# A decoder's row norms: statistics of four token sets per row group instead of two

## What is computed

```python
def _layernorm(x, axis=-1, eps=1e-05):
    m = jnp.mean(x, axis=axis, keepdims=True)
    v = jnp.var(x, axis=axis, keepdims=True)
    return (x - m) / jnp.sqrt(v + eps)
...
    x = x + _L0_attn_ref(_layernorm(x, axis=-1), ...)
    x = x + _L0_xattn_ref(_layernorm(x, axis=-1), ctx_1024, ...)
    x = x + _L0_ffn_ref(_layernorm(x, axis=-1), ...)
...
    x = x + _L3_ffn_ref(_layernorm(x, axis=-1), ...)
```

## Time and profile before

| | us |
|---|---|
| median of 3 runs | 2486.11 (2483.11 to 2487.94) |
| the profiled execution | 2487.08 |
| its span in the trace | 2485.0 |
| PE busy | 1851.5 (75%) |
| DVE busy | 1760.5 (71%) |
| ACT busy | 1120.0 (45%) |
| POOL busy | 707.7 (28%) |

### The profile page before, as it was taken

How to read it: one execution, slowest core, us unless ns; L and a number is a source line. 1 busy time by engine, 2 the same in 40 slices (tenths; PEclk the granted TensorE clock), 3 DMA queues, 4 the chain that set the end, 5 groups by cost and what they waited for, 6 DMA issues and landing times. The chain is left out here.

```text
span 2485.0 us, 36889 instructions
## 1 busy us (share of the span) xinstructions
PE 1851.5 (75%) x11751; PEld 1096.4 (44%) x11763; DVE 1760.5 (71%) x5601; ACT 1120.0 (45%) x3109; POOL 707.7 (28%) x617
## 2 busy tenths in 40 slices
PE   6996889962887999979887875666555555556778
PEld 2654446441354766644454543333333333333343
DVE  4336352268775666657745778999999999997665
ACT  3653442251315777731232554555555555554411
POOL 1200044005433333310032421344333333331130
PEclk7998899976998999989997897666665665667979
DMA  5000000310000000000100000000000000000000
GB/s 214 2 1 1 29 26 27 104 65 1 2 2 1 2 2 1 0 1 0 72 24 1 1 1 1 1 1 1 1 1 1 1 1 1 1 1 1 1 0 18
DMA packets 10591, 37.76 MB, mean 15 GB/s; under 512 B 1344, under 2 KB 7488, under 8 KB 9136
## 3 DMA queue, kind: packets, MB, share of 16 engines
q1 hardware_dynamic: 8880, 33.04, 3.4%
q0 software_dynamic: 1536, 2.59, 0.4%
HBM read 30.15 MB, written 5.51 MB: 14 GB/s over the span
## 5 line engine op out<-in xcount | busy, mean ns | idle before, releaser
L3733 PE MATMUL psum<-work 32*128 32x256 f32 x512 | 130.3, 653 | 288.2 <-ACT work L3851 288.2
L3913 DVE MATCH_REPLACE8 work<-work 128x256 f32<-128x256 f32 x768 | 322.1, 497 | 0.0
L3976 POOL TENSOR_TENSOR work<-work 128x1024 f32<-128x1024 f32 x63 | 148.3, 2355 | 484.2 <-ACT work L3851 484.2
L3910 DVE MAX8 work<-work 128x8 f32<-128x256 f32 x768 | 283.0, 495 | 0.0
L3733 PEld LDWEIGHTS psum<-work 32*128 32x128 f32 x512 | 77.8, 310 | 314.4 <-ACT work L3851 159.1
L718 POOL TENSOR_TENSOR work<-work 128x256 f32<-128x256 f32 (+2 forms) x144 | 133.5, 946 | 226.2 <-DVE work L1006 226.2
L934 ACT ACTIVATE work<-work 128x128 f32<-128x128 f32 (+1 forms) x320 | 145.3, 457 | 19.9 <-DVE work L981 18.2
L3851 ACT ACTIVATE work<-work 128x256 f32<-128x256 f32 x256 | 129.0, 504 | 0.0
L3913 DVE MATCH_VALUE_LOAD work<-work 128x8 f32 x768 | 128.0, 167 | 0.0
L3758 PE MATMUL psum<-work,tiles 128*8 128x256 f32 x512 | 116.9, 609 | 8.2 <-ACT work L3861 7.4
L3978 POOL TENSOR_TENSOR work<-work 128x1024 f32<-128x1024 f32 x63 | 119.3, 1894 | 6.0 <-DVE work L3935 1.2
(11 more groups left out here) (621 smaller groups left out, 4647.3 us busy)
## 6 DMA issues: line engine op xcount, KB each, us to landing
big_weights<-L0f_dram SPq DMA_DIRECT2D x1, 6117.5 KB, 28.5
big_weights<-L_dram SPq DMA_DIRECT2D x1, 5772.0 KB, 17.1
big_weights<-L_dram SPq DMA_DIRECT2D x1, 4952.5 KB, 16.1
choice_rows<-tiles SPq DMA_DIRECT2D x2, 1024.0 KB, 10.2
tiles<-choice_rows SPq DMA_DIRECT2D x8, 256.0 KB, 4.9
big_weights<-L_dram SPq DMA_DIRECT2D x1, 2027.0 KB, 21.2
big_weights<-L_dram SPq DMA_DIRECT2D x1, 1630.5 KB, 13.2
big_weights<-L0f_dram SPq DMA_DIRECT2D x1, 1630.5 KB, 6.2
```

Of the source, the lines that this page charges most:

```text
L3733: mm = nc.tensor.matmul(scores(n)[:, u, :], qb[head, tile % 2, u % 2 * P:(u % 2 + 1) * P], kb[head, tile % 2, :], start=True, stop=True, t ...
L3910: ch.step(v.max(top8[:, n % 2, u, r, :], src[:, u, :]))
L3913: ins = v.match_replace(raw[:, n % 2, u, :], top8[:, n % 2, u, r, :], src[:, u, :], REPLACED)
L3976: ch.link(g.tensor_tensor(mine, mine, rest[:, n % 2], ALU.subtract))
```

## The change

The number of token sets per row group becomes a constant, SETS = 4, in place of 2. Q becomes 64 columns, a set fills 8 rows of its group in place of 16, and the factor at the scaling follows. Roots and reciprocals work on 128 x 64; there are twice as many products of sums and of spreads, each with 64 columns. The two weight tables grow by 64 and 256 words a row.

```diff
+SETS = 4
...
     HF = CH // 2
-    Q = HF // 2
+    Q = HF // SETS
     sq, std, inv, warm = a.take(N), a.take(2, Q), a.take(2, Q), a.take(1)
...
-                    for s in range(2):
+                    for s in range(SETS):
                         mm = nc.tensor.matmul(c.psum[group[n], stats[pair], 0:Q], average_of[:, s, :],
-                                              sq[:, quarter(4 * pair + n, s)], start=(s == 0), stop=(s == 1),
+                                              sq[:, quarter(4 * pair + n, s)], start=(s == 0), stop=(s == SETS - 1),
                                               tile_position=(0, n * G))
                 mm.then_inc(c.var_ready.sem, 1)
...
             def spread_part(n, factors):
-                for s in range(2):
+                for s in range(SETS):
                     mm = nc.tensor.matmul(c.psum[:, spread[n], s * Q:(s + 1) * Q], value_of[group[n % 4], s, :],
...
-                nc.vector.scalar_tensor_tensor(dst[:, part[n]], (kept_in if kept else src)[:, part[n]], float(2 * P // G),
+                nc.vector.scalar_tensor_tensor(dst[:, part[n]], (kept_in if kept else src)[:, part[n]], float(SETS * P // G),
                                                c.psum[:, spread[n], 0:HF], ALU.mult, ALU.mult) \
...
-    half_of = np.arange(P // NC) // (P // NC // 2)
-    L.add(sm, "average_of", np.broadcast_to((half_of == np.arange(2)[:, None]).astype(np.float32) / P, (P, 2, P // NC)))
-    L.add(sm, "value_of", np.broadcast_to((np.tile(half_of, NC)[:, None] == np.arange(2)).astype(np.float32)[:, :, None] / P,
-                                          (P, 2, P)))
+    set_of = np.arange(P // NC) // (P // NC // SETS)
+    L.add(sm, "average_of", np.broadcast_to((set_of == np.arange(SETS)[:, None]).astype(np.float32) / P, (P, SETS, P // NC)))
+    L.add(sm, "value_of", np.broadcast_to((np.tile(set_of, NC)[:, None] == np.arange(SETS)).astype(np.float32)[:, :, None] / P,
+                                          (P, SETS, P)))
```

More of the change, by code:

```diff
@@ L372, in scale_also @@
                 dve.wait_ge(c.spread.sem, c.spread.at(2 * NC + n + 1))
-                nc.vector.scalar_tensor_tensor(also[0][:, part[n]], also[0][:, part[n]], float(2 * P // G),
+                nc.vector.scalar_tensor_tensor(also[0][:, part[n]], also[0][:, part[n]], float(SETS * P // G),
                                                c.psum[:, spread[n], 0:HF], ALU.mult, ALU.mult) \
```

## The result

The changed kernel takes 2555.66 us (2552.57 to 2556.49, 4 runs) where the kernel before, run beside it, takes 2487.03: a ratio of 1.027, 95% interval 1.0253 to 1.0286. It is slower by 69 us. The forecast was 2492.5 with a range up to 2506. Slower was the likelier sign, but the size is over ten times the forecast's, and the rival called "slower by far" came nearest.

The account below looks back on a forecast made before the run. The prediction took the norms' chain of waits, a strict relay, as the bound. Plain norms 0.6, with products 2.0, half-clock 2.2, first 0.7, clock-losing 0.6, load 0.4 gave +6.5 us: median 2492.5, range 2484 to 2506.

Parts of the forecast that it names:

- slower by far: Rival: PE doesn't look far enough ahead, sums' column groups no longer run beside each other; 2508 or about 2538, chance 0.10.
- Roots and reciprocals: Two of each on a norm's path, 64 columns instead of 128: -0.08 us for roots, -0.80 for reciprocals a norm.
- The price of a product: Spreads: weight load sets the pace, 64 columns cost as much as 128; +0.40 us, paid twice. Sums: level within 0.02.
- The faster rival: Rival: a 64-column product costs half, so spreads keep their length; -0.72 us a norm, 2473.5 us, chance 0.05.
- the fourth group should begin 80 to 120 ns late: Sums, four products of a column group together: lag less the shorter tail, +0.08 us each, +0.16 a norm.
- what a norm gains or loses the kernel gains or loses: All 18 norms, together 138.42 us: each a block of its own, the rest of the kernel not touched.
- No piece of it runs beside another piece of the same norm: One norm: a strict relay of PE sums, ACT root, DVE reciprocal and PE spreads, run twice.
- the spreads in between: First pair's last two spreads double, but the second root and reciprocal run beside them: no cost.
- plain norms: Seven norms ending with the last scaling: +0.08 us each at full clock, 0.6 us in all.
- half-clock norms: Two norms (1319.57, 1337.40) run mostly at 1.2 GHz: +1.0 to 1.1 us each, 2.2 us together.
- The rival by the clock: Longer bursts keep PE at full clock in three norms' last spreads, about 1 us each: 2489.5, chance 0.05.
- The load: Start of the kernel: small_weights grows by 160 KB and lands later, +0.4 us, with nothing covering it.

Follow-up runs that it names:

- half the columns: Kernel before, with roots and reciprocals on the first 64 of their 128 columns, products unchanged in number and width: 2479.84 us, ratio 0.9972.
- longer norms: Kernel before, with each of a norm's two reciprocals computed once more into an unused place ahead of the one used: 2531.80 us, ratio 1.0183.
- sets in turn, copy moved: Changed kernel with sums and spreads in turn over the parts and ACT's copy of chunk 2 ahead of the second root: 2497.20 us, ratio 1.0046.

## Why the prediction was wrong, step by step

**Roots and reciprocals: right.** -0.04 and -0.40 us each were forecast; 0.055 and 0.400 were measured, and with nothing else changed a norm became 0.87 us shorter (forecast 0.88).

**The price of a product: right.** Loads of one row group pace the spreads at 0.112 us, with 64 columns as with 128, so a burst of two lasts 1.11 instead of 0.72 us: +0.39 for a forecast of +0.40. Sums go at 0.056 us a record and stay level: 0.65 against 0.66. The faster rival, spreads at half price, is out.

**The failed step: the order of the products in PE's queue.** For the sums the forecast had "the fourth group should begin 80 to 120 ns late". It began 0.76 us late, three times 0.25. For the spreads it had no lag at the first burst and at most 0.22 us for the fourth group of the last one; there each group begins 0.50 us after the one ahead of it. The row that spoke against the rival, four groups starting within 40 ns behind twelve records, was of runs of two products, four records, which is what PE takes of one group without holding up others. It said nothing of runs of four; that "nothing in this kernel puts four products of a column group together now" was the warning, and a chance of 0.10 was too low for it. The rival was too small as well: it priced the sums alone (2508 or 2538), and the spreads lost about as much: 0.5 us at the first burst, 0.5 at the last, and 0.95 more before the products that wait for all parts.

**That "what a norm gains or loses the kernel gains or loses": wrong.** With half the columns the norms gave 16.0 us and the kernel 6.6, and with longer norms the kernel lost some 10 us more than they did. The sum put the price of the clock behind the norms at nothing. That "No piece of it runs beside another piece of the same norm" is a misreading of smaller weight: before the change DVE's first scalings, at 2475.94, already ran beside the second sums.

**"Nothing" for the spreads in between: right in the plain norms, by a hair.** PE gets to the last spreads just as their reciprocal ends (0.06 us to spare). In the two half-clock norms they do hold them up: the last spreads start 0.82 us after their reciprocal. ACT's copies, which the sum does not name, are late only in the runs that take parts in turn, where a norm took 7.56 us until a copy was moved, then 7.07.

**Half-clock norms:** forecast +1.0 to 1.1, measured +5.2 each (16.55 and 15.22 against 11.30 and 9.96); in turn 12.10 and 10.78, +0.8, near the forecast. The miss is the queue again.

**The rival by the clock: wrong sign.** It had longer bursts keep the full clock. The clock fell in more norms, not fewer (16 of 18 against 11), and the stretches behind them took longer.

**The load: sized a little low**, 0.5 by itself and 0.96 in the changed kernel, where 0.4 was forecast.

With the queue out of the way (sets in turn, copy moved) a plain norm ends 0.15 us below the one before, where the forecast was 0.08 above, and the kernel at 2497, inside the forecast's range, but by luck, on another road: its norms gain 1.4 us, and all else takes 9 more.

## What to carry to other kernels

Products that are to run beside each other in different row or column groups are best put in turn in the program; how many of one group may stand in a row (two did little harm here, three and four did) has to be read from the trace for that very number, not taken over from a shorter run. Putting parts in turn also puts their waits together: all of them then wait for the last bank to come free. And before a step is made shorter, count in the granted clock of what follows: of 16 us saved in these norms only 6.6 reached the kernel.

## What was not expected of the hardware

- PE held three records of a busy group before it stopped what stood behind (second group at 0.01, 0.14, 0.25 us for runs of two, three and four float32 products in the sums, 0.01, 0.28, 0.50 in the spreads).
- The granted clock is part of the price of these norms. It fell to 0.50, mostly some 5 to 10 us after the first sum, in 11 norms before, in all 18 where reciprocals were doubled, and in all 18 where the sums alone were put in turn. Shorter norms did not keep it either: with half the columns all else still took 9 us more. Which edit keeps it could not be settled.
- The pattern repeated itself within 0.3 us from the third norm on in one more execution of the unchanged kernel. With 160 KB more in the load, one stretch of 268 us with the same instructions took 6.5 us longer; one execution does not show whether the half microsecond at the start did it.
